# A two-layer attention and feed-forward kernel: layer 0's projections in another order, all of x asked for at once, its feed-forward weights loaded later and made ternary in group 6

## The reference

```python
qkv = x @ w_qkv                                   # 16 heads of 16
dots = einsum('bhid,bhjd->bhij', q, k) * scale    # scale = 0.25
attn = softmax(where(causal_mask, -inf, dots))
x = layernorm(x + (attn @ v) @ w_out + b_out)
# each of the three feed-forward weights:
scale = mean(abs(w)) + 1e-8
wq = clip(round(w / scale), -1, 1) * scale
x = layernorm(x + (silu(x @ wu.T) * (x @ wg.T)) @ wd.T)
```

## Time and profile before

| | |
|---|---|
| device time, median of 3 runs | 1011.0 us |
| lowest and highest | 1010.37 and 1013.32 us |
| the profiled execution: time, span | 1011.03 us, 1009.3 us |
| busy: PE, DVE, ACT, POOL | 949.5, 693.9, 589.7, 347.0 us |
| mean granted clock of PE | 0.983 |

### The profile page before, as it was taken

The page is one execution under the profiler, slowest core; times in us unless marked ns, Lnnn a source line. Parts: engine busy times, 40 slices in busy tenths (PEclk is TensorE's granted clock), DMA queues, the critical chain, the costliest instruction groups (busy, mean ns, idle before and its releaser), DMA issues. The chain is left out here.

```text
span 1009.3 us, 18025 instructions
## 1 busy us (share of the span) xinstructions
PE 949.5 (94%) x6546; PEld 515.2 (51%) x6546; DVE 693.9 (69%) x1535; ACT 589.7 (58%) x1204; POOL 347.0 (34%) x418
## 2 busy tenths in 40 slices
PE   6698999999998999978899999999999998999997
PEld 4352333333354887653334343443434354798896
DVE  2879888888834676677888888888888633433423
ACT  3444777777766335524577777777777768222321
POOL 3031322231123444322337363342625233224332
PEclk9898999999999999998799999999999999999999
DMA  7653211122000200241705062230401000000001
GB/s 245 196 172 107 65 49 43 44 59 64 2 1 19 76 1 8 77 151 48 213 9 176 4 173 72 64 109 28 134 2 40 2 1 1 1 1 22 22 1 42
DMA packets 32996, 64.20 MB, mean 64 GB/s; under 512 B 6095, under 2 KB 22367, under 8 KB 30532
## 3 DMA queue, kind: packets, MB, share of 16 engines
q1 hardware_dynamic: 31564, 58.47, 18.9%
q0 software_dynamic: 1072, 3.80, 1.1%
q10 hardware_dynamic: 272, 0.79, 0.2%
HBM read 50.45 MB, written 12.32 MB: 62 GB/s over the span
## 5 line engine op out<-in xcount | busy, mean ns | idle before, releaser
L1126 ACT ACTIVATE prob<-ps 128x512 f32<-128x512 f32 (+6 forms) x896 | 426.6, 541 | 159.8 <-PE ps L1171 156.7
L1171 PE MATMUL ps<-qop,kop 98*128 98x512 bf16 (+14 forms) x1376 | 271.5, 288 | 1.6 <-ACT prob L1126 0.6
L1157 PE MATMUL ps<-kop,qop 96*128 96x512 bf16 (+3 forms) x896 | 243.8, 357 | 20.9 <-DVE maxes L1056 15.4
L1171 PEld LDWEIGHTS ps<-qop,kop 107*128 107x128 bf16 (+1 forms) x1376 | 113.5, 97 | 212.6 <-ACT prob L1126 118.9
L1200 PE MATMUL ps<-prob,vst 128*32 128x512 f32 (+4 forms) x1792 | 211.2, 543 | 4.7 <-POOL prob L993 2.9
L1056 DVE CUSTOM_DVE_ANT_0 sums<-ps,tri 128x128 bf16<-128x128 f32 (+7 forms) x256 | 180.6, 754 | 20.0 <-PE ps L1157 18.5
L993 POOL TENSOR_TENSOR prob<-prob,keep 128x384 int32<-128x384 int32 (+2 forms) x144 | 121.6, 853 | 191.1 <-ACT prob L1126 190.9
L1056 DVE CUSTOM_DVE_ANT_0 sums<-ps,table 128x960 bf16<-128x960 f32 x128 | 148.0, 1156 | 47.6 <-PE ps L1157 35.4
L1601 PE MATMUL ps<-xs,wffn 128*128 128x512 f32 x640 | 156.2, 397 | 0.9 <-PEq L805 0.9
L1056 DVE CUSTOM_DVE_ANT_0 tri<-ps,table 128x960 bf16<-128x960 f32 x128 | 147.5, 1152 | 1.8 <-PE ps L1157 1.7
L1496 POOL TENSOR_TENSOR hs<-hf,hs 128x512 fp32r<-128x512 f32 x64 | 82.9, 1296 | 151.0 <-ACT hs L1519 142.7
(11 more groups left out here) (103 smaller groups left out, 684.4 us busy)
## 6 DMA issues: line engine op xcount, KB each, us to landing
table<-in_table SPq DMA_DIRECT2D x32, 464.0 KB, 4.7
qop<-q_parts SPq DMA_DIRECT2D x96, 128.0 KB, 2.6
kop<-k_parts SPq DMA_DIRECT2D x48, 128.0 KB, 2.6
kop<-k_parts SPq DMA_DIRECT2D x48, 96.0 KB
q_parts<-qop SPq DMA_DIRECT2D x8, 384.0 KB, 4.0
q_parts<-kop SPq DMA_DIRECT2D x8, 384.0 KB, 2.6
x<-in_x SPq DMA_DIRECT2D x4, 512.0 KB, 5.8
k_parts<-qop SPq DMA_DIRECT2D x4, 384.0 KB, 2.7
```

Of the source, the lines that this page charges most:

```text
L1126: nc.scalar.activation(prob[0:rows, q % 2, k % HG, lo % CH:lo % CH + hi - lo], ps[0:rows, home["exp", n, k], lo % CH:lo % CH + hi - lo], A ...
L1157: last = nc.tensor.matmul(ps[:, S_BANK + score_slot(L, k)[0] + a // CH, a % CH:a % CH + b - a], qop[0:RD, par, h, i0:i0 + P], kop[0:RD, pa ...
L1171: return nc.tensor.matmul(ps[:, bank, a % CH:a % CH + b - a], lhs, rhs, start=start, stop=True, skip_group_check=True)
```

## The change

Six edits, all of layer 0:

1. Batch 0's order becomes turns, units 0 to 3, v 0, units 4, 5, v 1, units 6, 7, v 2. v 3 moves in between the maxima of group 0. All steps of the opening use four banks (4 to 7) and no longer three.
2. Chunks 2 and 3 of x are asked for right behind the first two, not behind group 0's operands.
3. SP sends units 10 and 11 ahead of group 1's operands too, not behind them.
4. Batch 1's steps are dealt out by the width of the maxima, with 0.6 for a turn, not by their number.
5. POOL asks for the feed-forward weights when group 0's operands have landed. The three sums of absolute values go behind units 12, 13 and 14; total and thresholds go behind the first `rows` step. Total uses bank 6, which the first values of group 0 write, so those wait for the thresholds.
6. The ternary weights are made in group 6, in twelve slices of 128x512. POOL makes each slice's first comparison (three behind each of quads 8 to 11), DVE the second comparison with the subtraction, with `raw` and `below` both in SBUF. Twelve slices share eight places for the first result.

```diff
+        if group == N - 2 and n >= nq - 4:
+            steps += [("ternary", 3 * (n - nq + 4) + k, 0) for k in range(3)]
...
-PE_SHARE = ({"turn": 1, "unit": 1, "v": 1}, {"turn": 0.85, "unit": 1.72, "v": 1.72})
+PE_SHARE = ({"turn": 0.6, "unit": 1, "v": 1}, {"turn": 0.85, "unit": 1.72, "v": 1.72})
...
-        first = proj.steps(0)
-        for j, step in enumerate((("unit", 2), ("unit", 4), ("v", 2))):
-            first.insert(first.index(step), ("abs", j))
-        at = first.index(("unit", 6))
-        first[at:at] = [("total", 0), ("threshold", 0), ("ternary", 0)]
-        first += [("ternary", 1), ("ternary", 2)]
-        out = [(what, k, 0) for what, k in first]
-
-    width = [hi - lo for _, _, lo, hi in units] if layer.index == 1 else [1] * len(units)
+        out = [(what, k, 0) for what, k in proj.steps(0)]
+
+    width = [hi - lo if layer.index == 1 else hi - lo + 2 * P for _, _, lo, hi in units]
...
-        banks = ((4, 5, 6), (4, 5, 6)) if i == 0 else ((6, 7), (6, 7, 4, 5))
+        banks = ((4, 5, 6, 7), (4, 5, 6, 7)) if i == 0 else ((6, 7), (6, 7, 4, 5))
...
+        if self.i == 0 and b == 0:
+            return [*t, u[0], u[1], f[0], u[2], f[1], u[3], f[2], f[3], v[0], u[4], u[5], f[4], v[1], u[6], f[5], u[7], f[6],
+                    v[2], f[7]]
         if self.i == 0:
...
+            return [("v", TB // 2 - 1), *t, u[0], u[1], f[0], v[0], u[2], f[1], u[3], f[2], v[1], u[4], f[3], ("abs", 0),
+                    u[5], f[4], v[2], ("abs", 1), u[6], f[5], ("abs", 2), u[7], f[6], v[3], f[7]]
...
+        elif what == "ternary":
+
+            j, cols, home = self.slice_of(k)
+            pool.wait_ge(self.tern, 3 + (k - 7 if k >= 8 else 0))
+            nc.gpsimd.tensor_scalar(self.below[:, home], self.raw[j][:, cols], self.thr[:, 1, j:j + 1], None, ALU.is_lt
+                                    ).then_inc(self.below_set, 1)
...
+            dve.wait_ge(self.tern, 3)
+            dve.wait_ge(self.below_set, k + 1)
+            nc.vector.scalar_tensor_tensor(out=K.wffn[:, j, 0, cols], in0=self.raw[j][:, cols],
+                                           scalar=self.thr[:, 0, j:j + 1], in1=self.below[:, home].bitcast(F32),
+                                           op0=ALU.is_gt, op1=ALU.subtract).then_inc(self.tern, 1)
...
+                for c in range(NC // 2, NC):
+                    sp.dma_start(K.x[:, CT * c:CT * c + CT, :], xv[:, CT * c:CT * c + CT, :]
+                                 ).then_inc(proj.x_loaded[c], 16)
...
-            later = len(proj.units) // 2 + 2 * (1 - i)
+            later = len(proj.units) // 2 + 4 * (1 - i)
...
+            if i == 0:
+                pool.wait_ge(loaded[0], 16 * operands.loads)
+                for j, wt in enumerate(dram.ffn[0]):
+                    wt = wt.rearrange("(k p) n -> p k n", p=P)
+                    pool.dma_start(proj.raw[j].rearrange("p (k n) -> p k n", k=wt.shape[1]), wt
+                                   ).then_inc(proj.ffn_loaded, 16)
...
+                        elif k == 0 and i == 0:
+
+                            pe.wait_ge(proj.tern, 1)
```

More of the change, by code:

```diff
@@ L269, in opening_of @@
         due = work * sum(width[:n + 1]) / sum(width[:-2])
-        if layer.index == 0:
-            due = -(-work * (n + 1) // (len(units) - 2))
         while at < len(behind) and given + behind[at][2] <= due + 1e-6:
@@ L276, in opening_of @@
     out += [(what, k, 0) for what, k, _ in behind[at:]]
-    return out + [("parts", 0, 1), ("rows", 0, 1)] + [("max", k, 2) for k in range(AHEAD[layer.index])]
+    scale = [("total", 0, 0), ("threshold", 0, 0)] if layer.index == 0 else []
+    return out + [("parts", 0, 1), ("rows", 0, 1)] + scale + [("max", k, 2) for k in range(AHEAD[layer.index])]
 BRIDGE = {14: [("weigh", 0), ("decay", 0)],
@@ L362, in __init__ @@
             self.raw = [K.raw[:, j, :] for j in range(3)]
-            self.below = prep.xs[:].rearrange("p r s k c -> p (r s k c)")[:, 0:KD * E]
+            self.below = prep.xs[:].rearrange("p r s k c -> p (r s k c)")
+            self.below_set = sem("below_set")
             self.units = [(b, m, c) for b in range(B) for p in range(KD) for c in range(2) for m in (p, KD + p)]
@@ L410, in steps @@
         turns = [("turn", n) for n in range(b * turned, (b + 1) * turned)]
-        if self.i == 0:
-            vs = [("v", v) for v in range(b * 4, b * 4 + 4)]
-            out = [*turns]
-            for j in range(4):
-                for _, u in units[2 * j:2 * j + 2]:
-                    out += [("unit", u), ("finish", u - 1)] if u >= 1 else [("unit", u)]
-                out.append(vs[j])
-            return out if b == 0 else out + [("finish", len(self.units) - 1)]
-        u, t, f = units, turns, [("finish", k) for _, k in units]
+        u, t, f = units, turns, [("finish", k) for _, k in units]
+        v = [("v", k) for k in range(b * TB // 2, (b + 1) * TB // 2)]
+        if self.i == 0 and b == 0:
+            return [*t, u[0], u[1], f[0], u[2], f[1], u[3], f[2], f[3], v[0], u[4], u[5], f[4], v[1], u[6], f[5], u[7], f[6],
+                    v[2], f[7]]
+        if self.i == 0:
+            return [("v", TB // 2 - 1), *t, u[0], u[1], f[0], v[0], u[2], f[1], u[3], f[2], v[1], u[4], f[3], ("abs", 0),
+                    u[5], f[4], v[2], ("abs", 1), u[6], f[5], ("abs", 2), u[7], f[6], v[3], f[7]]
         return [*t[:4], u[0], u[1], f[0], ("weigh", 3), ("decay", 3), u[2], f[1], *t[4:6], f[2], ("divide", 3), ("scale", 3),
@@ L425, in beside_maxima @@
         if self.i == 0:
-            return [*self.steps(1)[:-1], ("finish", len(self.units) - 1, 1)]
+            return self.steps(1)
         first, second = self.steps(1)[:2], self.steps(1)[2:]
@@ L561, in act @@
                 act.wait_ge(self.abs_sum, k)
-            nc.scalar.activation(self.below, self.raw[k], ACT.Abs, accum_out=self.wsum[:, k:k + 1]
+            nc.scalar.activation(self.below[:, 0:KD * E], self.raw[k], ACT.Abs, accum_out=self.wsum[:, k:k + 1]
                                  ).then_inc(self.abs_sum, 1)
@@ L643, in dve, with slice_of @@
         elif what == "ternary":
[L644 to L650 removed]
+            j, cols, home = self.slice_of(k)
+            dve.wait_ge(self.tern, 3)
[3 more added lines that the diff above has]
+                                           op0=ALU.is_gt, op1=ALU.subtract).then_inc(self.tern, 1)
+    def slice_of(self, k):
+        parts = self.SLICES // 3
+        return k // parts, slice(k % parts * CH, (k % parts + 1) * CH), slice(k % 8 * CH, (k % 8 + 1) * CH)
     def bank(self, what, k):
@@ L709, in pe @@
             pe.wait_ge(self.ones_set, 1)
-            nc.tensor.matmul(ps[:, self.SIDE, 0:3], K.ones[:], self.wsum[:], start=True, stop=True).then_inc(self.total, 1)
+            self.wait_read(pe, *self.last_on[self.TOTAL])
+            nc.tensor.matmul(ps[:, self.TOTAL, 0:3], K.ones[:], self.wsum[:], start=True, stop=True).then_inc(self.total, 1)
 class Operands:
@@ L891, in _ @@
             operands.load(sp, 0)
-            if i == 0:
-                for c in range(NC // 2, NC):
-                    sp.dma_start(K.x[:, CT * c:CT * c + CT, :], xv[:, CT * c:CT * c + CT, :]
-                                 ).then_inc(proj.x_loaded[c], 16)
-            later = len(proj.units) // 2 + 2 * (1 - i)
+            later = len(proj.units) // 2 + 4 * (1 - i)
             for u in range(4, later):
@@ L944, in _ @@
                 pool.wait_ge(proj.x_loaded[1], 16)
-                for j, wt in enumerate(dram.ffn[0]):
-                    wt = wt.rearrange("(k p) n -> p k n", p=P)
-                    pool.dma_start(proj.raw[j].rearrange("p (k n) -> p k n", k=wt.shape[1]), wt
-                                   ).then_inc(proj.ffn_loaded, 16)
                 pool.dma_start(K.identb[:], dram.identb).then_inc(K.tri_loaded, 16)
@@ L1225, in step @@
                         pe.wait_ge(m_cut, n + 1)
-                        if n == 0 and i == 1:
+                        if n == 0:
                             proj.wait_read(pe, *proj.last_on[SIDE])
```

14 lines of the change are left out of this document (5 added, 9 removed).

## The result

The changed kernel is slower, and by more than the forecast's range allowed: a median of 1020.96 us (1016.69 to 1023.81, 6 runs) against 1011.77 us (1010.37 to 1014.34, 6 runs) for the kernel before. The ratio is 1.0095, with a 95% interval of 1.0077 to 1.0114. Its profiled execution took 1016.69 us (span 1015.0), the lowest of its six, so I later took a second trace of the same kernel, at 1021.15 us (span 1019.4), near the median.

What follows compares the result with a forecast made beforehand. PE, busy 94% of the span, was taken as the bound, so edits pay only where it waits. 1011.03 - 8.2 (front) + 9.1 (group 6: 7.6 + 0.3 + 1.2) = 1011.9, forecast 1012 us, range 1004 to 1018.

Steps and rivals of the forecast that it cites:

- The front: Opening to the first exponential's product: 8.7 us earlier rows less 0.5, so 8.2 us gained, bounds 5 and 9.5.
- 1.7 less: Group 0's maxima: if the first turns still run at half clock, the gain at rows is 1.7 us smaller.
- I take 0.67 (the mask's, and a little for the operand), with 0.60 and 1.30 as ends: Group 6: price in us of each of POOL's twelve 128x512 comparison slices, 12 x 0.67 = 8.0 us.
- Each adds about 0.55 less the 0.1 that start-up hides: 0.44: Group 6: POOL and DVE take turns at SBUF, each DVE slice delaying POOL 0.44 us, 11 x 0.44 = 4.8 us.
- Gather and clock, 1.5: Group 6: gather behind DVE's last slice, 0.3 us, and PE at half clock after waiting, 1.2 us lost.
- The dear comparison: Rival, group 6: POOL's slice costs as much as a two-input instruction, masks 15.2 us late, 1019.5 us; 15 in 100.
- take-over: Group 6: POOL and DVE alternate at SBUF, the waiting one going first; 0.44 us for each of eleven slices, 4.8 us.
- Overlap: Rival, group 6: DVE's slices don't hold POOL up, mask 2.8 us late, clock stays, 1005.6 us; 30 in 100.
- The half front: Rival, opening: late group 1 operands or x's chunks taking transfers leave about half of the 8.2, 1016 us; 12 in 100.

## Why the prediction was wrong

- **The front: right.** Fourth send 21.02 (forecast 21.5), first maximum 33.80 (33.9), rows 70.85 (71.9), first exponential 74.10 (75.7) in the first trace; in the second the rows' send comes 3.4 later, 2.8 of it with the clock at 0.50 behind the first maximum. The gain at the rows' send is 9.8 or 6.4 us, around the forecast 8.2. I had left half clock there as "1.7 less". It cost 2.8 from first maximum to rows' send (40.43 against 37.58), and it was the more frequent case, four of the six traces with this opening.
- **"I take 0.67 (the mask's, and a little for the operand), with 0.60 and 1.30 as ends": this step failed.** The slice took 1.57, outside both ends. The nearest rows I chose, copy and mask, were of the same shape but of other forms, and the form decides. The upper end was taken from the two-input instruction in the belief that one input can't cost more; it does. The tensor-scalars of POOL in the trace were no wider than 4 columns and told their start-up alone. Twelve slices became 18.8 us instead of 8.0. The 0.77 us that the Trainium skill has for a tight loop over 512 elements (GPSIMD Engine Reference, "Elementwise — side-by-side cycle accounting") is half of what this form took, 1.57.
- **"Each adds about 0.55 less the 0.1 that start-up hides: 0.44": right in size, wrong in number, and the error goes the other way.** It held at three slices of eleven (1.2 us in all instead of 4.8), those that began while DVE's step ran. DVE's step beside a slice under way took 1.10 for 0.75, and POOL didn't slow. The Trainium skill (SBUF — State Buffer, "Who interferes with whom") has the second to issue blocked until the first finishes. This pair doesn't bear that out: DVE's step began 0.16 us behind the slice and ended 0.3 us ahead of its end. For a cheap slice the 0.44 would have come up oftener, as two of the three copies show with 1.06 for 0.61: the two terms weren't independent. With the measured prices the forecast's own sum gives 18.8 + 1.2 + 2.4 - 7.6 = 14.8 for the 14.55 measured.
- **Gather and clock, 1.5: too low.** 2.5 in the first trace, as PE's clock stayed at 0.50 for some 5 us of full work behind the wait and not for 2 to 3. The gather itself cost nothing there: PE goes from quad 0's values (289.68) to its turn (291.54) without a wait.
- **Rivals.** The dear comparison was what happened, at 15 in 100, and its 1019.5 lies inside the runs. It came out right by two errors: 1.30 for 1.57 and a take-over that came three times and not eleven. Overlap was nearly right in its mechanism and had the wrong price of a slice. The half front didn't come: also with the clock at 0.50 the front gave 6.4 of the 8.2, and group 1 began on time (0.5 us lost to group 6 in one trace, none in the other).
- **The sum.** 1011.03 - 9.8 + 0.5 + 17.1 - 2.1 = 1016.7 for the first trace's 1016.69; 1011.03 - 6.4 - 0.1 + 16.3 + 0.4 = 1021.2 for the second's 1021.15 (its T is 89.43, and its last stretch 688.0 for 687.6). The range ended at 1018 because the upper price did.

What stays open: whether the clock falls in a wait of 3.4 us differs between executions of one program, and no run shows what decides it. The same holds for how long it stays down behind the rows step. The 4.7 us of spread in what follows layer 1's weights weren't taken apart. Of the front's edits the order of the units and the transfers were undone by themselves; the fourth bank, units 10 and 11 ahead of group 1's operands and the dealing out by width were not.

## What to carry to other kernels

Take an instruction's price from a row of the same form (engine, operation, operands) before one of the same shape; where the trace has none, the upper bound isn't the dearest neighbour, and an edit whose sign hangs on that price is best settled by a run with the one instruction. Work for an "idle" engine goes where nothing waits behind it: twelve slices cost 17 us between masks, and eight of them nothing in quads 4 to 7. And before work is put on an engine, name what is queued behind it there, with the whole price of the work in front of it (here the gather, worth 8.7 us of T). Fill waits of PE with work that is due anyway: here 1.9 us of work went into the wait, and the half clock that could follow the longer wait cost 2.8.

## What the runs showed of the hardware

- POOL, 128x512, fp32 in SBUF to SBUF: tensor-scalar 1.56 to 1.59 us for a comparison or a product with a per-partition scalar, 1.49 for a comparison with an immediate; copy or cast 0.61; affine select 0.63 to 0.64; two-input tensor-tensor 1.30. One-input arithmetic was the dearest of them.
- The same comparison on DVE takes 0.48 us, three times less, and the two-input second step 0.75. Where DVE's comparison and an affine select of POOL overlap, the first takes up to 0.86 and the mask 0.71 to 1.01 instead of 0.64.
- POOL beside DVE's second step: what POOL begins while the step runs takes 0.3 to 0.45 us more, in all three forms seen (tensor-scalar 2.00 for 1.57, cast 1.06 for 0.61, affine select 1.08 for 0.63); what is under way when the step begins isn't slowed, and the step takes 1.00 to 1.10 instead of 0.75.
- Behind a PE wait of 3.3 to 3.5 us the granted clock was 1.00 in two traces (both 3.50 us) and at or near 0.50 for 4 to 7 us in four others (3.29 to 3.47 us) of nearly the same program; behind the waits of 4.43, 4.62, 5.53 and 7.50 us it had fallen each time; behind 0.92, 1.65 and 1.77 not, behind 1.99 it had. Behind the 2.0 to 2.25 us at the first rows step it was at 0.50 in all fourteen traces, for 6 to 13 us.
